# The last batch's end of a first attention inside the next block's programs, and low parts on another engine

## The chip, the cores and the metric

The kernel runs on one core of one Trainium2 chip. A core has TensorE (matrix products and transposes, results in PSUM), VectorE, ScalarE and GpSimd, each with its own program, and SyncE, whose queue starts the transfers. The engines meet at semaphores. The metric is the device time of one execution in microseconds (us), lower is better. In the profile PE is TensorE's matmuls, PEld its weight loads, DVE VectorE, ACT ScalarE, POOL GpSimd, SP SyncE.

## What is computed

Four transformer layers over 16 batches of 128 tokens, in float32. Layer 0 is an attention with 16 heads of 8 over 256 positions a batch and 128 channels, and a feed-forward. Layer 1 lets latents attend to the context and to themselves, with 16 heads of 16. Layer 2 has two cross attentions with 16 heads of 128. Layer 3 has a causal and a cross attention with 16 heads of 16. Cut to the parts that the change touches:

```python
# layer 0, per batch: q from x, k and v from the context
x = x + softmax(q @ k.T / sqrt(8)) @ v @ Wo
x = x + gelu(layer_norm(x) @ W1 + b1) @ W2 + b2
# layer 1
k, v = split(concat(context, x) @ kv_w + kv_b)
x = rmsnorm(x + softmax(q @ k.T / 4 + mask) @ v @ out_w + out_b)
# layers 1, 2 and 3, at their ends
x = x + gelu(norm(x) @ w1 + b1) @ w2 + b2
```

## The kernel before

Each attention and each feed-forward is one block: a set of five engine programs. All engines meet between two blocks. Inside a block there are only semaphores.

**The order of the work in a block** is one list of steps (`Order`), and each engine's program runs those steps of the list that are its own, in the order of the list. In the attentions of layers 0, 1 and 3 the list is made by sorting: a table (`AT0`, `AT1`, `AT3`) gives each stage a time in units of one batch, a step's key is its batch plus that time (`order0`, `order1`), and of equal keys the one that the table names first goes first. In layer 1 the second half of a batch's exponents has -3.18 (`exponents`, four steps for each half), and the next batch's turned maxima, `neg_T_a`, have -4.18, so the two keys are equal but for rounding. In the list `neg_T_a` of the next batch stands behind the second half for batches 0 to 7 and ahead of it for batches 8 to 14. PSUM banks go round in rings (`Ring`), one bank for each job in the order of TensorE's steps.

**Layer 0's attention** (`attention0`) ends for each batch with a chain: `untangle` (8 transposes of the slots, L1146), `share` (divide by the sum, L1311 and L1315), `context_T` (2 transposes) and its copy `turned_T`, `out` (one product with Wo, L1160), `added` (plus the tokens, L1322), `back` (2 transposes, L1167) and its copy `back_a` (L1254), `stats_b`, `root_b` (GpSimd), `scaled_b` (L1344), `renormed` (2 transposes, L1174) and `renormed_a`, which writes the normalized tokens `nT` (L1260).

**Layer 0's feed-forward** (`feed_forward0`) goes over eight groups of 512 tokens, two batches of 256 each. VectorE splits the group's `nT` into a rounded high part and the rest (`split`, L259 and L261), TensorE multiplies twice with three products each (`up`, L114), ScalarE makes Gelu (L242), TensorE multiplies back (`down`, L224), VectorE adds to x (`add`, L267) and, in groups 1 to 4, makes the masks for layer 1. TensorE's order is up(0), then up(g + 1), down(g).

**The feed-forwards of layers 1 to 3** (class `Feed`, order `FEED_ORDER`) have four groups g of four batches. A product of two float32 matrices is made of three products of high and low parts. So ScalarE rounds quarters of the weights (`w1_high` L1871, `w2_high` L1877) and the rest is made as low part: `w1_low(0)` on VectorE (L1971), `w1_low(1..3)` (L1919) and `w2_low(0..3)` (L1924) on GpSimd. Then for each of eight f: `up` on TensorE (six products of 512 columns), `gelu` on ScalarE (high part L1886, full L1889), `h_split` on VectorE (`h_low`, L1981). Then four steps `down(g, n)` of 24 products each, every one followed by `added` on VectorE (L1989), which needs `biased(b)` of its batch: GpSimd adds the bias row to x (L1948), with no wait but, in layers 2 and 3 at batch 12, for the scaled tokens. In layers 2 and 3 the normalization of the last group's tokens is made inside the block (`late_...`: statistics, root on GpSimd, scaling L2025, two turns L2069), and in layer 2 also that of group 0 for the layer behind (`early_...`: `early_stats` and `early_root` after `up(1, 1)`, `early_scaled` L2016 after `up(1, 4)`, in the list ahead of the last three `h_split` of group 1). Layer 2 takes its token parts from the attention and makes no `split`. In layer 1 GpSimd runs `split_context` after its steps of the list (L2713 and L2716, each twice, 2048 columns), for layer 2. At the end of every block GpSimd clears the semaphores of the block before (`clear_stale`). In the page's and the trace's names `l_mlp_...` stands for the feed-forwards' tiles.

## Time and profile before

| what | us |
|---|---|
| median of three runs (2301.53 to 2304.23) | 2302.02 |
| the profiled execution, its own time | 2303.46 |
| its span, from first to last instruction | 2301.4 |
| PE busy (share of the span) | 2161.2 (94%) |
| PEld busy | 1793.4 (78%) |
| DVE busy | 1479.8 (64%) |
| ACT busy | 1277.5 (56%) |
| POOL busy | 684.6 (30%) |

The blocks lie in the span like this: layer 0's attention to 328, its feed-forward to 358, layer 1's attention to 610, its feed-forward to 714, layer 2's attentions to 1786, its feed-forward to about 1890, layer 3's attentions to 2196, its feed-forward to the end at 2301.

A share is a mean over stretches with different limits, so it is only a first look. The timeline gives for each instruction or merged row of instructions its start, its duration, engine, line, operation, tiles with shapes and count, and in brackets how long the engine was idle before it and what it waited for. Rows of one engine alone merge otherwise than rows of all. `PEq` as releaser is the meeting of the engines between blocks. Matmul ends are modelled; the start of the next is the safer number.

### The profile page before, as it was taken

How to read it: one execution, taken by the hardware profiler on the slowest of the kernel's cores; microseconds unless marked ns; L12 is line 12 of the kernel's file. 1: busy time of each engine (PE TensorE's matmuls, PEld its weight loads, DVE VectorE, ACT ScalarE, POOL GpSimd, SP SyncE). 2: the span in 40 equal slices, each digit the busy share in tenths (PEclk: the TensorE clock that was granted, in tenths of full speed). 3: DMA queues.
4: the chain of work that ended last, by engine and by line, in shares of the span. 5: the costliest groups of instructions: out<-in, count | busy, mean ns of one | idle time of the engine just before them, and what ended most of it. 6: DMA issues, size and time to landing. Idle time of an engine off the chain costs nothing. (4 is left out here: it accounts for less than half of the span.)

```text
span 2301.4 us, 47738 instructions
## 1 busy us (share of the span) xinstructions
PE 2161.2 (94%) x18208; PEld 1793.4 (78%) x18208; DVE 1479.8 (64%) x2807; ACT 1277.5 (56%) x3300; POOL 684.6 (30%) x682
## 2 busy tenths in 40 slices
PE   6999979998798999999999999999998899999889
PEld 4666646877687888888888888888887786776678
DVE  5888744555454765666666666666666539999963
ACT  4777754555534444444445444444444448888853
POOL 5344310111433422030303312030101507677740
PEclk9999999999899999999999999999999999999999
DMA  3000020000102000010100001000000210000000
GB/s 133 16 16 11 2 56 1 2 2 2 38 1 78 24 24 24 10 38 1 47 1 19 29 17 31 10 28 1 1 1 32 79 35 23 2 2 2 2 10 28
DMA packets 33661, 50.58 MB, mean 22 GB/s; under 512 B 2592, under 2 KB 22048, under 8 KB 32416
## 3 DMA queue, kind: packets, MB, share of 16 engines
q1 hardware_dynamic: 33440, 47.53, 6.9%
q8 instruction: 151, 2.47, 0.5%
q14 instruction: 70, 0.57, 0.1%
HBM read 45.43 MB, written 2.10 MB: 21 GB/s over the span
## 5 line engine op out<-in xcount | busy, mean ns | idle before, releaser
L690 ACT ACTIVATE l_probs<-l_s_psum,l_neg_max 128x129 f32<-128x129 f32 x512 | 181.7, 368 | 267.7 <-DVE l_neg_max L753 267.7
L777 DVE TENSOR_TENSOR x<-x,l_o_psum 128x512 f32<-128x512 f32 x256 | 176.2, 688 | 189.9 <-PE l_o_psum L644 187.9
L522 POOL TENSOR_TENSOR l_head_w_high<-l_head_raw,one 128x768 fp32r<-128x768 f32 x30 | 44.5, 1483 | 516.9 <-PE l_o_psum L644 516.9
L675 ACT ACTIVATE l_KT<-l_k_psum,cols 128x512 f32<-128x512 f32 x128 | 88.2, 689 | 198.0 <-PE l_k_psum L114 198.0
L1303 DVE TENSOR_REDUCE l_neg_max<-l_psum 128x2 f32<-128x512 f32 x256 | 163.5, 683 | 46.5 <-PE l_psum L1093 46.2
L2365 POOL TENSOR_TENSOR l_probs<-l_probs,l_mask_add 128x512 f32<-128x512 f32 x128 | 161.9, 1287 | 76.2 <-DVE l_probs L2593 76.2
L644 PE MATMUL l_o_psum<-l_head_w_high,l_context_low 128*128 128x256 f32 x512 | 155.6, 304 | 8.8 <-DVE l_context_low L758 8.8
L758 DVE SCALAR_TENSOR_TENSOR l_context_low<-l_c_psum,cols,l_context_high 128x512 fp32r<-128x512 f32 x128 | 95.8, 749 | 105.5 <-ACT l_context_high L682 104.7
L2535 ACT ACTIVATE l_probs<-l_probs,l_neg_max 128x128 f32<-128x128 f32 x512 | 159.8, 396 | 5.4 <-DVE l_neg_max L2600 5.0
L1232 ACT ACTIVATE l_PT<-l_psum 128x512 f32<-128x512 f32 x256 | 132.2, 602 | 54.6 <-PE l_psum L1121 54.6
L644 PE MATMUL l_o_psum<-l_head_w_high,l_context_high 128*128 128x256 f32 x512 | 144.4, 282 | 5.1 <-DVE x L777 3.1
L630 PEld LDWEIGHTS l_c_psum<-l_PT,values 128*128 128x128 f32 x1024 | 134.4, 192 | 12.5 <-DVE l_PT L749 1.9
L644 PE MATMUL l_o_psum<-l_head_w_low,l_context_high 128*128 128x256 f32 x512 | 143.5, 280 | 0.0
L768 DVE TENSOR_TENSOR values<-l_v_psum,l_value_rows 128x512 f32<-128x512 f32 x128 | 88.5, 691 | 84.8 <-PE l_v_psum L114 83.4
L630 PE MATMUL l_c_psum<-l_PT,values 128*128 128x128 f32 x1024 | 136.0, 276 | 0.9 <-DVE l_PT L749 0.8
L610 PE MATMUL l_s_psum<-l_KT,l_QT 128*128 128x129 f32 x1024 | 135.8, 275 | 0.8 <-ACT l_QT L669 0.8
L1886 ACT ACTIVATE l_mlp_h_high<-l_mlp_psum,cols 128x512 fp32r<-128x512 f32 x96 | 66.3, 690 | 121.3 <-PE l_mlp_psum L114 114.8
L1981 DVE TENSOR_TENSOR l_mlp_h_low<-l_mlp_h,l_mlp_h_high 128x512 fp32r<-128x512 f32 x96 | 87.3, 924 | 69.3 <-ACT l_mlp_h L1889 69.1
L669 ACT ACTIVATE l_QT<-l_q_psum,l_query_bias 128x512 f32<-128x512 f32 x128 | 88.3, 690 | 76.6 <-PE l_q_psum L114 76.6
L610 PEld LDWEIGHTS l_s_psum<-l_KT,l_QT 128*128 128x128 f32 x1024 | 124.8, 191 | 1.4 <-ACT l_QT L669 1.2
L114 PE MATMUL l_mlp_psum<-l_mlp_w_high,l_mlp_h_high 128*128 128x256 f32 x384 | 111.7, 291 | 8.3 <-DVE l_mlp_h_low L1981 8.3
L114 PE MATMUL l_v_psum<-l_value_w_high,ctx_high 128*128 128x512 f32 x256 | 112.3, 439 | 7.5 <-DVE l_value_w_low L798 6.8
(303 smaller groups left out, 6403.0 us busy)
## 6 DMA issues: line engine op xcount, KB each, us to landing
l_head_raw<-in_l_heads SPq DMA_DIRECT2D x32, 384.0 KB, 3.1
l_w<-in_l_w SPq DMA_DIRECT2D x4, 1024.0 KB, 9.9
l_ctx_in<-in_ctx_T SPq DMA_DIRECT2D x16, 256.0 KB, 5.4
l_value_raw<-in_l_values SPq DMA_DIRECT2D x8, 512.0 KB, 3.6
l_value_rows<-in_l_rows SPq DMA_DIRECT2D x8, 512.0 KB, 5.2
l_x_in<-in_x_T SPq DMA_DIRECT2D x16, 128.0 KB, 2.2
l_x_in<-in_ctx_T SPq DMA_DIRECT2D x16, 128.0 KB, 2.5
values<-in_l_w SPq DMA_DIRECT2D x2, 1024.0 KB, 6.2
```

The lines of the kernel that those rows point to most:

```text
L114: last = pe.matmul(out, left[a], right[b], start=(start and n == 0), stop=(stop and n == 2))
L610: last = pe.matmul(scores[:, i // 2, i % 2, :], QT[:, i * S:(i + 1) * S], KT[:, i, :], start=True, stop=True)
L630: last = pe.matmul(c_bank[:, i * S:(i + 1) * S], V[:, u % 2, i, hh * P:(hh + 1) * P], PT[:, i * S:(i + 1) * S], start=True, stop=True)
L644: last = pe.matmul(o_bank[:, i % 2 * D:(i % 2 + 1) * D], context[left][:, i * S:(i + 1) * S], wo[right], start=(m == 0), stop=(m == 2))
L690: last = act.activation(probs[:, i, :], scores[:, i // 2, i % 2, :], ACT.Exp, bias=neg_max[:, i:i + 1], scale=1.0, accum_out=den[:, i:i + 1])
L758: dve.scalar_tensor_tensor(out=context[1][:, :], in0=c_bank[:, :], scalar=vector("bias_v", s), in1=context[0][:, :].bitcast(F32), op0=ALU. ...
L768: dve.tensor_tensor(out=V[:, u % 2, i, :], in0=v_bank[:, :], in1=value_rows[:, u // 4 % 2, 0, :], op=ALU.add).then_inc(v_free, 1)
L777: dve.tensor_tensor(out=x, in0=x, in1=o_bank[:, :], op=ALU.add).then_inc(o_free, 1)
L1232: act.activation(PT[:, 2 * w + t, g, :], score_banks[g][:, :], ACT.Exp).then_inc(exp_done, 1)
L1303: dve.tensor_reduce(neg_max[:, u % 2, qt, at:at + 2], bank[:, :].rearrange("p (e k) -> p e k", e=2), AX, ALU.max, negate=True).then_inc(fr ...
L2365: pool.tensor_tensor(out=probs[:, s % SCORES3, :, :], in0=probs[:, s % SCORES3, :, :], in1=four(mask_add[:, mask_slot(u), :]), op=ALU.add) ...
L2535: last = act.activation(p, p, ACT.Exp, bias=neg_max[:, s % SCORES3, m:m + 1], scale=1.0)
```

## The change

1. Layer 0's attention no longer has the last batch's steps from `untangle` on (`ENDING0`). They stand in `feed_forward0`, in a new class `Ending0`, with two further PSUM banks: TensorE untangles after up(0), turns the context after down(0), multiplies by Wo after down(1), turns back after down(2), turns the normalized tokens after down(4). ScalarE copies after its steps of groups 1, 3 and 5, VectorE's and GpSimd's steps are between theirs, and the split of the last group waits for the normalized tokens. The slots and the tokens live on in SBUF for it.
2. In layer 1's attention the second half of the exponents has -3.2 instead of -3.18, so it stands ahead of the next batch's `neg_T_a` for every batch. No other engine's order changes.
3. In the three `Feed` blocks all low parts of the weights are made on VectorE: `w1_low` where they stood, `w2_low(0..3)` after the `h_split` of f = 1 to 4 of group 0. One semaphore fewer.
4. GpSimd's `biased` of a group's first batch waits until the group's last up (f = 7) is done. Everything behind it in GpSimd's program waits with it: in layer 2 `late_low`, `early_root`, in layer 1 `split_context`.

```diff
--- before.py
+++ after.py
+class Ending0:
...
+    def untangle(self, pe):
+        for qt, bank in enumerate((self.first, self.second)):
+            for j in range(4):
+                at = j % 2 * 2 * S + qt * P
+                last = pe.transpose(bank[:, j * P:(j + 1) * P], self.c.slots0[:, j // 2, at:at + P], self.c.ident[:, :])
+            last.then_inc(self.untangled, 1)
+
+    def context_T(self, pe):
+        pe.wait_ge(self.shared, 2)
+        for qt in range(2):
+            last = pe.transpose(self.first[:, qt * P:(qt + 1) * P], self.ctx_q[:, qt, :], self.c.ident[:, :])
+        last.then_inc(self.context_turned, 1)
+
+    def make_out(self, pe):
+        pe.wait_ge(self.ctx_T_done, 1)
+        pe.matmul(self.second[:, 0:2 * S], self.c.w["l0_wo"][:, 0, :], self.ctx_T[:, :], start=True, stop=True)\
+            .then_inc(self.out_made, 1)
...
+    def copy_ctx_T(self, act):
+        act.wait_ge(self.context_turned, 1)
+        act.activation(self.ctx_T[:, :], self.first[:, 0:2 * S], ACT.Copy).then_inc(self.ctx_T_done, 1)
...
+    def share(self, dve):
+        for qt, bank in enumerate((self.first, self.second)):
+            dve.wait_ge(self.untangled, qt + 1)
+            slot = bank[:, :].rearrange("p (j m n) -> p m j n", j=4, m=4)
+            by_head = self.rden[:, qt, :, :].rearrange("p (m j) n -> p m j n", m=4)
+            dve.reciprocal(by_head, slot[:, :, :, 8:9]).then_inc(self.rden_done, 1)
+            dve.wait_ge(self.rden_done, qt + 1)
+            dve.tensor_tensor(out=self.ctx_q[:, qt, :].rearrange("p (m j d) -> p m j d", m=4, j=4),
+                              in0=slot[:, :, :, 0:8], in1=by_head.to_broadcast([P, 4, 4, 8]), op=ALU.mult)\
+                .then_inc(self.shared, 1)
...
+    def root(self, pool):
+        pool.wait_ge(self.var_done, 1)
+        inverse_root(pool, self.c, self.rstd_part, 0, self.mean_var[:, :, 1:2], self.rstd[:, :, :], 1e-5, 2)\
+            .then_inc(self.rstd_done, 1)
...
             up(0)
+            ending.untangle(pe)
             for g in range(groups):
                 if g + 1 < groups:
                     up(g + 1)
                 down(g)
+                if g == 0:
+                    ending.context_T(pe)
+                if g == 1:
+                    ending.make_out(pe)
+                if g == 2:
+                    ending.back(pe)
+                if g == 4:
+                    ending.renormed(pe)
...
+                if g == 1:
+                    ending.copy_ctx_T(act)
+                if g == 3:
+                    ending.copy_back(act)
+                if g == 5:
+                    ending.norm(act)
...
+            ending.root(pool)
...
+                if g == groups - 1:
+                    dve.wait_ge(ending.normed, 1)
...
             split(0)
             split(1)
+            ending.share(dve)
             for g in range(groups):
                 if g + 2 < groups:
                     split(g + 2)
+                if g == 4:
+                    ending.scale(dve)
                 add(g)
+                if g == 1:
+                    ending.add(dve)
+                if g == 3:
+                    ending.statistics(dve)
                 if 1 <= g < 5:
                     c.ahead1.masks(dve, masks_loaded, g - 1)
...
+ENDING0 = ("untangle", "share", "context_T", "turned_T", "out", "added", "back", "back_a", "stats_b", "root_b", "scaled_b",
+           "renormed", "renormed_a")
...
         for stage, at in AT0.items():
+            if u == B - 1 and stage in ENDING0:
+                continue
...
-        tokens = sb("tokens", [P, 4, 2 * KEYS])
+        tokens = c.tokens0
...
-    "exponents": (-4.15, -4.11, -3.97, -3.97, -3.18, -3.18, -3.18, -3.18),
+    "exponents": (-4.15, -4.11, -3.97, -3.97, -3.2, -3.2, -3.2, -3.2),
...
-        self.w1_first = sem("w1_first")
...
     def gpsimd(self, pool):
-        def w1_low(q):
-            if q == 0:
-                return
-            raw, high, low = self.quarter1(q)
-            pool.wait_ge(self.w1_rounded, q + 1)
-            pool.tensor_tensor(out=low, in0=raw, in1=high.bitcast(F32), op=ALU.subtract).then_inc(self.w1_ready, 1)
-
-        def w2_low(q):
-            raw, high, low = self.quarter2(q)
-            pool.wait_ge(self.w2_rounded, q + 1)
-            pool.tensor_tensor(out=low, in0=raw, in1=high.bitcast(F32), op=ALU.subtract).then_inc(self.w2_ready, 1)
-
...
         def biased(b):
             x = self.c.x[:, b, :]
+            if b % 4 == 0:
+                self.filled(pool, "up", b // 4, 7)
             if self.late and b == 12:
                 pool.wait_ge(self.xn_done, 1)
...
         def w1_low(q):
-            if q == 0:
-                raw, high, low = self.quarter1(0)
-                dve.wait_ge(self.w1_rounded, 1)
-                dve.tensor_tensor(out=low, in0=raw, in1=high.bitcast(F32), op=ALU.subtract).then_inc(self.w1_first, 1)
+            raw, high, low = self.quarter1(q)
+            dve.wait_ge(self.w1_rounded, q + 1)
+            dve.tensor_tensor(out=low, in0=raw, in1=high.bitcast(F32), op=ALU.subtract).then_inc(self.w1_ready, 1)
+
+        def w2_low(q):
+            raw, high, low = self.quarter2(q)
+            dve.wait_ge(self.w2_rounded, q + 1)
+            dve.tensor_tensor(out=low, in0=raw, in1=high.bitcast(F32), op=ALU.subtract).then_inc(self.w2_ready, 1)
 
...
         def up(g, f):
-            if f < 2:
-                pe.wait_ge(self.w1_first, 1)
-            else:
-                pe.wait_ge(self.w1_ready, f // 2)
+            pe.wait_ge(self.w1_ready, f // 2 + 1)
...
 FEED_ORDER = [("split", 0, 0), ("w1_high", 0), ("w1_low", 0), ("split", 0, 1), ("late_stats",)]
 for _q in range(1, 4):
     FEED_ORDER += [("w1_high", _q), ("w1_low", _q)] + ([("late_root",)] if _q == 1 else [])
-for _q in range(4):
-    FEED_ORDER += [("w2_high", _q), ("w2_low", _q)]
+FEED_ORDER += [("w2_high", _q) for _q in range(4)]
 for _g in range(4):
     FEED_ORDER += [("biased_b2", 4 * _g + _n) for _n in range(4)]
     for _f in range(8):
         FEED_ORDER += [("up", _g, _f), ("gelu", _g, _f), ("h_split", _g, _f)] + LATE_AT.get((_g, _f), [])
+        FEED_ORDER += [("w2_low", _f - 1)] if _g == 0 and 1 <= _f <= 4 else []
...
-                    with nc.sbuf_tensor("pos", [P, 4, P], F32) as pos:
-                        c.pos = pos
-                        attention0(c)
                     with ExitStack() as one:
-                        c.ahead1 = Ahead1(c, lambda n, shape, dt=F32: one.enter_context(nc.sbuf_tensor(f"l1_{n}", shape, dt)))
-                        feed_forward0(c)
+                        with ExitStack() as zero:
+                            c.slots0 = zero.enter_context(nc.sbuf_tensor("l0_slots", [P, 2, BANK], F32, side="right"))
+                            c.tokens0 = zero.enter_context(nc.sbuf_tensor("l0_tokens", [P, 4, 4 * S], F32, side="right"))
+                            with nc.sbuf_tensor("pos", [P, 4, P], F32) as pos:
+                                c.pos = pos
+                                attention0(c)
+                            c.ahead1 = Ahead1(c, lambda n, shape, dt=F32:
+                                              one.enter_context(nc.sbuf_tensor(f"l1_{n}", shape, dt)))
+                            feed_forward0(c)
```

## Rows read from the trace of the kernel before

**Rows 1.** Timeline, ScalarE, end of first attention: start, duration, engine, line, operation [idle before].

```profile
318.90 0.38 ACT L1254 ACTIVATE l_r<-l_psum 128x256 f32<-128x256 f32 x1
...
323.75 0.39 ACT L1254 ACTIVATE l_r<-l_psum 128x256 f32<-128x256 f32 x1 [1.74 <-DVE l_rn L1344]
...
328.27 0.42 ACT L236 ACTIVATE l_mlp_w_high<-l_w 128x256 fp32r<-128x256 f32 x1 [0.29 <-PEq L892]
```

**Rows 2.** Windows, same place: length, busy PE, PEld, DVE, ACT, POOL, granted clock, DMA.

```profile
324.00:328.00 4.00, 0.93 (x4) 0.29 (x2) 1.35 (x6) 1.26 (x3) 0.89 (x2) 0.57 0.00 0
...
330.00:334.70 4.70, 4.62 (x11) 3.69 (x12) 2.26 (x4) 1.75 (x3) 2.89 (x7) 0.50 0.99 333
```

**Rows 3.** Timeline, TensorE, first feed-forward: one group's second product.

```profile
347.55 1.88 PE L224 MATMUL l_mlp_psum<-l_mlp_hT,l_w 128*128 128x512 f32 x4
```

**Rows 4.** Timeline, ScalarE, second layer's attention, batches 6 to 10 and 14.

```profile
460.33 2.42 ACT L1701 ACTIVATE l_PT<-l_psum,l_mask_col 128x512 f32<-128x512 f32 x4 [0.52 <-PE l_psum L1601]
...
468.65 2.06 ACT L1701 ACTIVATE l_PT<-l_psum 128x512 f32<-128x512 f32 x4 [1.99 <-PE l_psum L1601]
...
474.25 2.42 ACT L1701 ACTIVATE l_PT<-l_psum,l_mask_col 128x512 f32<-128x512 f32 x4 [0.73 <-PE l_psum L1601]
...
487.49 2.42 ACT L1701 ACTIVATE l_PT<-l_psum,l_mask_col 128x512 f32<-128x512 f32 x4 [0.52 <-PE l_psum L1601]
...
498.16 0.28 ACT L1693 ACTIVATE l_neg_T<-l_psum 128x128 bf16<-128x128 bf16 x1 [4.34 <-PE l_psum L1580]
...
503.85 2.42 ACT L1701 ACTIVATE l_PT<-l_psum,l_mask_col 128x512 f32<-128x512 f32 x4 [0.74 <-PE l_psum L1601]
...
517.74 2.42 ACT L1701 ACTIVATE l_PT<-l_psum,l_mask_col 128x512 f32<-128x512 f32 x4 [0.52 <-PE l_psum L1601]
...
586.27 0.28 ACT L1693 ACTIVATE l_neg_T<-l_psum 128x128 bf16<-128x128 bf16 x1 [3.98 <-PE l_psum L1580]
```

**Rows 5.** Timeline, TensorE and VectorE, layer 1's feed-forward and the next block's start.

```profile
615.47 0.79 PE L114 MATMUL l_mlp_psum<-l_mlp_n_high,l_mlp_w_high 128*128 128x512 f32 x1 [1.46 <-DVE l_mlp_n_low L1964]
...
643.05 14.89 DVE L1981 TENSOR_TENSOR l_mlp_h_low<-l_mlp_h,l_mlp_h_high 128x512 fp32r<-128x512 f32 x7 [2.27 <-ACT l_mlp_h L1889]
...
671.20 0.69 DVE L1981 TENSOR_TENSOR l_mlp_h_low<-l_mlp_h,l_mlp_h_high 128x512 fp32r<-128x512 f32 x1 [2.27 <-ACT l_mlp_h L1889]
...
704.71 0.42 DVE L1989 TENSOR_TENSOR x<-x,l_mlp_psum 128x256 f32<-128x256 f32 x1 [0.88 <-PE l_mlp_psum L114]
...
714.09 1.41 DVE L727 BATCH_NORM_STATS2 l_stats<-x 128x6 f32<-128x256 f32 x4 [0.32 <-PEq L2110]
```

**Rows 6.** Timeline, GpSimd, layer 1's feed-forward: the context split's first two steps.

```profile
637.53 3.60 POOL L2713 TENSOR_TENSOR ctx_high<-ctx_raw,one 128x2048 fp32r<-128x2048 f32 x1
...
641.22 4.62 POOL L2716 TENSOR_TENSOR ctx_low<-ctx_raw,ctx_high 128x2048 fp32r<-128x2048 f32 x1
```

**Rows 7.** Timeline, layer 2's feed-forward: TensorE, GpSimd, ScalarE.

```profile
1799.83 0.66 PE L2069 MATMUL l_mlp_psum<-ident,l_mlp_xn 128*128 128x128 f32 x4 [1.76 <-DVE l_mlp_xn L2025]
...
1809.12 2.83 POOL L1948 TENSOR_TENSOR x<-x,rows 128x256 f32<-128x256 f32 x4
...
1823.76 1.34 POOL L104 TENSOR_TENSOR l_mlp_rstd<-l_mlp_rstd,minus_half 128x4 f32<-128x4 f32 x1
...
1844.62 0.69 ACT L1886 ACTIVATE l_mlp_h_high<-l_mlp_psum,cols 128x512 fp32r<-128x512 f32 x1 [15.87 <-PE l_mlp_psum L114]
```

**Rows 8.** Timeline, layer 3's feed-forward: ScalarE and VectorE.

```profile
2201.41 0.69 ACT L1886 ACTIVATE l_mlp_h_high<-l_mlp_psum,cols 128x512 fp32r<-128x512 f32 x1
...
2209.05 9.18 DVE L1981 TENSOR_TENSOR l_mlp_h_low<-l_mlp_h,l_mlp_h_high 128x512 fp32r<-128x512 f32 x7
...
2230.52 0.69 ACT L1886 ACTIVATE l_mlp_h_high<-l_mlp_psum,cols 128x512 fp32r<-128x512 f32 x1 [13.62 <-PE l_mlp_psum L114]
...
2252.94 0.69 ACT L1886 ACTIVATE l_mlp_h_high<-l_mlp_psum,cols 128x512 fp32r<-128x512 f32 x1 [11.63 <-PE l_mlp_psum L114]
...
2296.39 0.42 DVE L1989 TENSOR_TENSOR x<-x,l_mlp_psum 128x256 f32<-128x256 f32 x1 [2.46 <-PE l_mlp_psum L114]
```

More of the change, by code:

```diff
@@ L188, in feed_forward0 @@
         n_parts = [sb(f"n_{n}", [P, 2, BANK], F32R) for n in ("high", "low")]
-        psum = [ctx.enter_context(nc.psum_tensor(f"l0_mlp_psum{i}", [P, BANK], F32)) for i in range(6)]
+        psum = [ctx.enter_context(nc.psum_tensor(f"l0_mlp_psum{i}", [P, BANK], F32)) for i in range(8)]
         up_banks, down_banks = psum[0:4], psum[4:6]
@@ L195, in feed_forward0 @@
         masks_loaded, ctx_loaded, ahead_made = sem("masks_loaded"), sem("ctx_loaded"), sem("ahead_made")
+        ending = Ending0(c, sb, sem, psum[6:8])
         ctx.callback(hand_over, c, held, sems)
@@ L918, in attention0 @@
         PT = sb("PT", [P, 4, 4, BANK])
-        slots = sb("slots", [P, 2, BANK])
+        slots = c.slots0
         rden = sb("rden", [P, 2, H, 1])
@@ L1948, in biased @@
             pool.tensor_tensor(out=x, in0=x, in1=self.c.row(self.finish), op=ALU.add).then_inc(self.x_biased, 1)
-        return {"w1_low": w1_low, "w2_low": w2_low, "biased_b2": biased, "late_root": late_root, "late_low": late_low,
+        return {"biased_b2": biased, "late_root": late_root, "late_low": late_low,
                 "early_root": early_root}
@@ L2029, in late_scaled @@
             last.then_inc(self.xn_done, 1)
-        return {"split": split, "w1_low": w1_low, "h_split": h_split, "added_b2": added, "late_stats": late_stats,
+        return {"split": split, "w1_low": w1_low, "w2_low": w2_low, "h_split": h_split, "added_b2": added, "late_stats": late_stats,
                 "late_scaled": late_scaled, "early_stats": early_stats, "early_scaled": early_scaled}
```

54 lines of the change are left out of this document (added).

## The prediction

> **What bounds the kernel now.** I first read the busy shares: TensorE is busy 94% of the span, so only the stretches where it waits, or works at half clock, can give anything back. The page's chain that ended last covers only the end, so I went to the timeline at each place that the diff touches.
>
> At the end of the first attention the reader is to see a chain of short steps with nothing beside it: batch 15's residual is copied back at 323.75, and ScalarE starts the feed-forward at 328.27; batch 14's was copied at 318.90 [rows 1]. TensorE's granted clock falls to its lower level there (0.57 on average over 324 to 328, 0.50 at the start of the feed-forward) [rows 2].
>
> In the second layer's attention I read when ScalarE starts the first-half exponents of each batch [rows 4]. Batches 6 to 8 start at 460.33, 474.25 and 487.49: 13.92 and 13.24, a pair in 27.16. Batches 8 to 10 start at 487.49, 503.85 and 517.74: 16.36 and 13.89, a pair in 30.25. From batch 8 on, `neg_T_a` of the next batch stands before the second-half exponents and waits 4.34 (3.98 in batch 14) for TensorE [rows 4].
>
> In the feed-forwards one undisturbed group of four batches takes 22.42 (2230.52 to 2252.94 in layer 3) [rows 8]. Layer 1's second group takes 28.15 from its first `h_low` to the next group's, and seven of its `h_low` take 14.89 where one alone takes 0.69 [rows 5]; GpSimd runs the context split beside them [rows 6]. Layer 3's first group takes 29.11, seven `h_low` 9.18 [rows 8]: GpSimd works on low parts and biases there.
>
> **First layer: minus 1.6.** Removed from the first attention: the last batch's end. Next late there is batch 14's end, of the same steps: 4.52 from its copy to the next block, so 318.90 + 4.52 = 323.42 instead of 328.27, 4.85 earlier [rows 1]. The feed-forward gets it on TensorE, which is the bound of that stretch: 14 transposes, at most 0.66 / 4 = 0.165 each (four took 0.66) [rows 7], 2.3; the output matmul, 256 columns, two passes of half of 1.88 / 4, 0.5 [rows 3]. `renormed` in group 4 waits for VectorE's add, statistics, masks, split of group 6 and scaling; I estimate 0.4 of waiting, since this chain is about as long as TensorE's up and down. Together 3.2, between 2 and 4.9. The half-clock start moves with the block [rows 2]: I take the same cost; TensorE idles less, so it could also save one or two. VectorE's `share` and `added` and ScalarE's copies lie beside TensorE's up; the new wait of the last split for `normed` holds only `add` of group 5 and the last up behind it, which TensorE reaches after one up and one down. GpSimd's root queues ahead of clearing semaphores only.
>
> **Second layer's order: minus 13.2.** For batches 8 to 14 the second-half exponents now go ahead of the next `neg_T_a`, as they already do in batches 0 to 7; all other engines keep their order. Behind them waits `neg_T_a`, and the next batch's score on TensorE for it; in batches 6 and 7 just this order runs in 27.16 a pair. From batch 8 to 13 that is three times 16.36 - 13.92 = 2.44 and twice 13.89 - 13.24 = 0.65: 8.6. Batches 13 and 14 have no further projections to fill with; between 0.65 and the wait of 3.98 I take 2.3 each, as the steady case with the long wait has 2.4. Sum 13.2, between 9.9 and 16.6 [rows 4].
>
> **Layer 1's feed-forward: plus 0.6.** (a) The low parts of the first weights leave GpSimd, so VectorE's second token split is not slowed and TensorE's wait of 1.46 goes [rows 5]; the uninterrupted start may bring full clock sooner. I take 2.3, between 0 and 3. The seven low parts cost VectorE 0.69 each, in gaps that it has beside ups of 1.36; without that cover 4.8. (b) GpSimd's biases wait for the last up of their group, and the context split, queued behind all of them, moves out of group 1: 28.15 - 22.42 = 5.7 gained [rows 5, 8]. (c) It now stands at the block's end. The last up ends one down step before the add at 704.71; three more steps end at 713.35, so a step is 2.88 and the up ends at 701.83, 12.26 before the next block's 714.09 [rows 5]. From there GpSimd needs 2.83 for four biases [rows 7], 2 x (3.60 + 4.62) = 16.4 for the split [rows 6], some 0.4 for gaps and 0.3 to the next block, and then, uncovered for the first time, the clearing of twenty semaphores. No row shows a clearing. After the last add (2296.39) there are 5.0 to the span's end, with one store and some thirty clearings [rows 8], so one costs at most 0.17; I take 0.05, 1.0 in all (0 to 3.4). Sum 20.9 against 12.26: 8.6 lost. The half clock of the next block's start is there already, as TensorE starts it after a pause either way. 8.6 - 5.7 - 2.3 = 0.6. The same bound over 29 clearings at the second attention's end, 16 of them new, could cost up to 2.4; I take nothing, since they lie beside the last normalization's chain.
>
> The Trainium skill, page SBUF — State Buffer, section Summary: rules for kernel authors, says that a VectorE instruction with two inputs in SBUF and a GpSimd instruction that reads SBUF exclude each other, and the one that issues second waits until the other ends. The 14.89 above agree. By that rule the first bias at the tail could wait for the last `h_low`, and the tail would cost up to 0.7 more than by the row of four biases.
>
> **Layer 2's feed-forward: plus 0.9.** The first group gets rid of TensorE's wait of 1.76 for the scaled tokens, which VectorE computes against GpSimd's low parts [rows 7], and of slowed `h_low`; I take 2.2, between 0 and 3. But `early_root` is queued on GpSimd behind the biases of group 1, which now wait for that group's last up. VectorE's `early_scaled` stands before three `h_low` and waits for it. Counted from the last up: four biases 2.83, root about 1.7 with its first add, four scalings of 0.42 (taken from the add at 704.71, of the same width), three `h_low` of 0.69, the last products 0.4: 8.7 where a down step is 2.88 [rows 5, 7]. That is 5.8 of waiting, most of it one pause, so some 1.5 of half clock after it: 7.3. Today this group is 15.87 - 11.63 = 4.24 long of the undisturbed one [rows 7, 8]. Plus 3.1, between 0 and 5; the cover of the biases elsewhere is the down phase, 11.5.
>
> **Layer 3's feed-forward: minus 5.0.** First group 29.11 - 22.42 = 6.7 too long [rows 8], 1.0 of it the two turns. VectorE then has per up only 0.69, and 0.69 more in four of them, plus four scalings at 0.42: it no longer bounds. Part of the rest is the half clock at the start, which stays; but the first split is quicker too. Between 2 and 6.5; I take 5.0, nearer to the excess. GpSimd's end is hidden here.
>
> **Sum.** -1.6 - 13.2 + 0.6 + 0.9 - 5.0 = -18.3. The profiled execution took 2303.46 (span 2301.4), 1.4 over the median of 2302.02. The profiled one would take 2285.2, the median 2283.7.
>
> **Rivals.**
> - GpSimd does not matter. The slow `h_low` come from ScalarE's pace, or VectorE's own low parts now bound the first groups. Then 2.3, 2.2 and 5.0 are not gained: 2283.7 + 9.5 = 2293.2. For it: VectorE was full in these groups. Against: 9.18 for seven, at 0.69 alone [rows 8]. 9%.
> - The attention's rhythm changes at batch 8 for another reason: 2283.7 + 13.2 = 2296.9. Against: the 4.34 wait stands just there, and nothing else in the order changes. 4%.
> - Held GpSimd queue costs more: clearings at 0.17 (2.4 here, 2.4 at the attention's end), layer 2's stall at 5 instead of 3.1: 2290.4. 8%.
> - Slower than before: `neg_T_a`, now behind the exponents' 2.06 [rows 4], holds the next score in all seven batches. It decides if TensorE reaches that score before `neg_T_a` is done; then seven times 2.06 = 14.4 are lost instead of 13.2 gained: 2283.7 + 27.6 = 2311.3. Against: batches 6 and 7. 2%.
>
> **How the numbers follow.** The forecast has 77%. Its range takes the bounds of the unknown costs, which hardly all fall on one side: 2276.5 to 2291; this takes in the third rival, and leaves out the other 15% and the far ends. A measurement here tells about 0.2% (4.6) from no change. All cases but the last are faster by more: with a little for mishaps, 95% faster, 3% the same, 2% slower.
>
> **What would show it.** Right: first exponents of batches 8 to 13 about 27.2 a pair; seven `h_low` near their own 0.69 in layer 3's first group; group 1 of layer 1 at 22.4; about 21 between its last up and the next block, with GpSimd alone at the end; a TensorE pause of 5 in layer 2's second group; the first feed-forward starting 4.9 earlier and lasting 3 longer. Wrong: pairs still at 30.25, or a first group still above 27.

## The result and the profile after

The changed kernel took 2285.52 us, median of 4 runs (2281.77 to 2286.55), beside 2302.62 for the kernel before on the same chip: a ratio of 0.9922 (95% interval 0.9905 to 0.9939). A second measurement, made together with the variants below, gave 2282.18 in 5 runs and 0.9913 (0.9900 to 0.9926). The forecast was 2283.7. The profiled execution took 2285.99, its span 2283.4, so 18.0 less than before's span; the sum in the prediction said 18.3.

Stretch by stretch, from block start to block start. The last column takes the mean length over the profiled kernels of this study that have the edit, less the mean over those that lack it: 8 and 4 for the first three rows; 3 and 3 for the others (the changed kernel, its repeat and e3 against before, e1 and e2), since the other six have half of the feed-forward's edit or more than all of it. The repeat's profile shows how far one kernel differs from itself: 1.8 in the second layer's attention, 0.7 in layer 1's first group and 1.5 in layer 2's second. I had expected under 0.3 in the groups.

| stretch | forecast | before, after | difference | over all profiles |
|---|---|---|---|---|
| start of the first feed-forward | -4.85 | 328.27, 323.54 | -4.7 | -4.8 |
| its length | +3.2 | 30.20, 31.99 | +1.8 | +1.9 |
| second layer's attention | -13.2 | 252.07, 238.73 | -13.3 | -15.3 |
| layer 1's feed-forward | +0.6 | 103.55, 104.54 | +1.0 | +0.8 |
| layer 2's attention | 0 | 1071.79, 1073.59 | +1.8 | +0.4 |
| layer 2's feed-forward | +0.9 | 105.96, 105.65 | -0.3 | +1.3 |
| third attention | 0 | 303.90, 304.37 | +0.5 | +0.8 |
| layer 3's feed-forward | -5.0 | 105.65, 100.96 | -4.7 | -4.2 |

Changed kernel, timeline of ScalarE (columns as in rows 1). The first lines answer to [rows 1], the others to [rows 4].

```profile
319.03 0.38 ACT L1392 ACTIVATE l_r<-l_psum 128x256 f32<-128x256 f32 x1
...
323.54 0.42 ACT L352 ACTIVATE l_mlp_w_high<-l_w 128x256 fp32r<-128x256 f32 x1 [0.29 <-PEq L1030]
...
486.13 2.42 ACT L1839 ACTIVATE l_PT<-l_psum,l_mask_col 128x512 f32<-128x512 f32 x4 [0.52 <-PE l_psum L1739]
...
496.81 0.28 ACT L1831 ACTIVATE l_neg_T<-l_psum 128x128 bf16<-128x128 bf16 x1 [0.29 <-PE l_psum L1718]
...
500.05 2.42 ACT L1839 ACTIVATE l_PT<-l_psum,l_mask_col 128x512 f32<-128x512 f32 x4 [0.73 <-PE l_psum L1739]
...
565.43 2.42 ACT L1839 ACTIVATE l_PT<-l_psum,l_mask_col 128x512 f32<-128x512 f32 x4 [0.52 <-PE l_psum L1739]
...
572.30 0.28 ACT L1831 ACTIVATE l_neg_T<-l_psum 128x128 bf16<-128x128 bf16 x1
```

Batch 14's copy to the next block is 4.51, as [rows 1] had it for batch 15. From batch 8 on `neg_T_a` comes behind the second-half exponents and waits 0.29 where it waited 4.34 [rows 4]; batches 8 and 9 start 13.92 apart.

Changed kernel, layer 1's feed-forward, timeline of VectorE: the answer to [rows 5].

```profile
624.51 0.69 DVE L2112 TENSOR_TENSOR l_mlp_h_low<-l_mlp_h,l_mlp_h_high 128x512 fp32r<-128x512 f32 x1 [2.27 <-ACT l_mlp_h L2026]
...
634.04 1.18 DVE L2112 TENSOR_TENSOR l_mlp_h_low<-l_mlp_h,l_mlp_h_high 128x512 fp32r<-128x512 f32 x1 [0.67 <-ACT l_mlp_h L2026]
635.14 0.94 DVE L2089 CAST l_mlp_n_high<-nT_early 128x512 fp32r<-128x512 f32 x1
636.12 1.11 DVE L2091 TENSOR_TENSOR l_mlp_n_low<-nT_early,l_mlp_n_high 128x512 fp32r<-128x512 f32 x1
...
690.22 0.42 DVE L2120 TENSOR_TENSOR x<-x,l_mlp_psum 128x256 f32<-128x256 f32 x1 [2.46 <-PE l_mlp_psum L114]
698.80 1.41 DVE L859 BATCH_NORM_STATS2 l_stats<-x 128x6 f32<-128x256 f32 x4 [8.16 <-PEq L2238]
```

The same stretch on GpSimd, the answer to [rows 6].

```profile
632.78 3.90 POOL L2075 TENSOR_TENSOR x<-x,rows 128x256 f32<-128x256 f32 x4 [18.90 <-PE l_mlp_psum L114]
...
678.38 3.71 POOL L2075 TENSOR_TENSOR x<-x,rows 128x256 f32<-128x256 f32 x4 [18.90 <-PE l_mlp_psum L114]
682.05 3.60 POOL L2841 TENSOR_TENSOR ctx_high<-ctx_raw,one 128x2048 fp32r<-128x2048 f32 x1
...
693.98 4.49 POOL L2844 TENSOR_TENSOR ctx_low<-ctx_raw,ctx_high 128x2048 fp32r<-128x2048 f32 x1
```

The context split no longer lies beside the `h_low`; it follows the last group's biases. The last add ends at 690.64, VectorE waits 8.16 for GpSimd, and TensorE's last product lies 8.6 before the next block. From the last up (678.3) to the next block it is 20.5, where I had worked out 20.9. GpSimd's last operation ends at 698.47 and the next block starts at 698.80, so the twenty semaphore clearings, priced at 1.0 and "uncovered", cost nothing. The trace has them, in the view of their source line:

```profile
L66 POOLq EVENT_SEMAPHORE_RANGE_CLEAR  x20: 44/44/44, 693.9 to 695.3; - x20
```

They are 0.07 apart, issued by GpSimd's sequencer (`POOLq`) while its engine works on the last `ctx_low` (693.98 to 698.47). The price of one was near, but they are covered. New, and not in the prediction: the first bias lies beside the group's last `h_low`, which takes 1.18 instead of 0.69.

Changed kernel, timeline of ScalarE: first `h_high` of group 1 in layer 1, of group 2 in layer 2, and of groups 1 and 2 in layer 3 (the answers to [rows 7] and [rows 8]).

```profile
623.22 0.69 ACT L2023 ACTIVATE l_mlp_h_high<-l_mlp_psum,cols 128x512 fp32r<-128x512 f32 x1 [12.01 <-PE l_mlp_psum L114]
...
1830.06 0.69 ACT L2023 ACTIVATE l_mlp_h_high<-l_mlp_psum,cols 128x512 fp32r<-128x512 f32 x1 [17.89 <-PE l_mlp_psum L114]
...
2211.44 0.69 ACT L2023 ACTIVATE l_mlp_h_high<-l_mlp_psum,cols 128x512 fp32r<-128x512 f32 x1 [11.39 <-PE l_mlp_psum L114]
...
2234.23 0.69 ACT L2023 ACTIVATE l_mlp_h_high<-l_mlp_psum,cols 128x512 fp32r<-128x512 f32 x1 [12.00 <-PE l_mlp_psum L114]
```

Undisturbed groups wait 12.01 instead of 11.63 and take 22.80 instead of 22.42. Layer 2's second group waits 17.89 where [rows 7] had 15.87. Why, GpSimd and VectorE show.

```profile
1810.94 2.80 POOL L2075 TENSOR_TENSOR x<-x,rows 128x256 f32<-128x256 f32 x4 [16.61 <-PE l_mlp_psum L114]
1813.70 0.20 POOL L102 TENSOR_TENSOR l_mlp_rstd<-l_mlp_mean_var,epsilons 128x4 f32<-128x4 f32 x1
1813.98 1.02 POOL L104 TENSOR_TENSOR l_mlp_rstd<-l_mlp_rstd,minus_half 128x4 f32<-128x4 f32 x1
```

```profile
1815.03 1.67 DVE L2147 SCALAR_TENSOR_TENSOR l_mlp_xn<-x,l_mlp_mean_var,l_mlp_rstd 128x256 f32<-128x256 f32 x4 [6.22 <-POOL l_mlp_rstd L104]
1816.62 1.89 DVE L2112 TENSOR_TENSOR l_mlp_h_low<-l_mlp_h,l_mlp_h_high 128x512 fp32r<-128x512 f32 x3
```

The root stands behind the held biases, VectorE waits 6.22 for it, and three `h_low` that TensorE's down needs stand behind that. TensorE's own pause is 4.80:

```profile
1817.45 0.55 PE L114 MATMUL l_mlp_psum<-l_mlp_w_high,l_mlp_h_high 128*128 128x256 f32 x1 [4.80 <-DVE l_mlp_h_low L2112]
```

### The profile page after: what moved, and what is told of

It is laid out like the page before. It is cut to its first block and busy times, and to the rows that moved or that the text cites. A ratio compares the mean times of both kernels' runs of the same rounds, so it can differ in the third digit from the quotient of the medians.

```text
span 2283.4 us, 47741 instructions
## 1 busy us (share of the span) xinstructions
PE 2156.4 (94%) x18208; PEld 1791.3 (78%) x18208; DVE 1465.7 (64%) x2828; ACT 1277.7 (56%) x3300; POOL 653.0 (29%) x661
## 5 line engine op out<-in xcount | busy, mean ns | idle before, releaser
L890 DVE SCALAR_TENSOR_TENSOR l_context_low<-l_c_psum,cols,l_context_high 128x512 fp32r<-128x512 f32 x128 | 95.8, 748 | 105.3 <-ACT l_context_high L814 104.5
L114 PE MATMUL l_v_psum<-l_value_w_high,ctx_high 128*128 128x512 f32 x256 | 112.8, 441 | 15.4 <-DVE l_value_w_low L930 14.8
L776 PEld LDWEIGHTS l_o_psum<-l_head_w_high,l_context_low 128*128 128x128 f32 x512 | 96.5, 188 | 26.8 <-DVE l_context_low L890 24.1
L2112 DVE TENSOR_TENSOR l_mlp_h_low<-l_mlp_h,l_mlp_h_high 128x512 fp32r<-128x512 f32 x96 | 71.0, 742 | 71.4 <-ACT l_mlp_h L2026 71.2
```

The lines of the kernel that those rows point to most:

```text
L114: last = pe.matmul(out, left[a], right[b], start=(start and n == 0), stop=(stop and n == 2))
L776: last = pe.matmul(o_bank[:, i % 2 * D:(i % 2 + 1) * D], context[left][:, i * S:(i + 1) * S], wo[right], start=(m == 0), stop=(m == 2))
L890: dve.scalar_tensor_tensor(out=context[1][:, :], in0=c_bank[:, :], scalar=vector("bias_v", s), in1=context[0][:, :].bitcast(F32), op0=ALU. ...
```

## The experiments

First the change in its three parts, each by itself in the kernel before.

**The order alone (e1_order).**

```
-    "exponents": (-4.15, -4.11, -3.97, -3.97, -3.18, -3.18, -3.18, -3.18),
+    "exponents": (-4.15, -4.11, -3.97, -3.97, -3.2, -3.2, -3.2, -3.2),
```

> The kernel before with one edit alone: the second-half exponents of the second layer go ahead of the next batch's neg_T_a from batch 8 on. Forecast: 13.2 us less than before (bounds 9.9 to 16.6), first-half exponents of batches 8 to 13 in 68.2 instead of 76.9, of 13 to 15 in 21.5 instead of 27.6. Rival 2 (the rhythm changes at batch 8 for another reason): no change, 76.9 stays. In the changed kernel's trace batch 1 to 2 of this attention was 1.6 longer than before; if that comes from what stands in front of it (the first feed-forward), this kernel does not have it and saves 14.8; if it comes from the order itself, it has it and saves 13.2.

Measured: 2287.21, 0.9930 of before (0.9917 to 0.9942), so 16.1 less (13.4 to 19.1). The attention takes 237.07. Its ScalarE timeline:

```profile
498.62 0.28 ACT L1693 ACTIVATE l_neg_T<-l_psum 128x128 bf16<-128x128 bf16 x1 [0.28 <-PE l_psum L1580]
...
567.23 2.42 ACT L1701 ACTIVATE l_PT<-l_psum,l_mask_col 128x512 f32<-128x512 f32 x4 [0.52 <-PE l_psum L1601]
574.11 0.28 ACT L1693 ACTIVATE l_neg_T<-l_psum 128x128 bf16<-128x128 bf16 x1
577.64 2.42 ACT L1701 ACTIVATE l_PT<-l_psum,l_mask_col 128x512 f32<-128x512 f32 x4 [0.74 <-PE l_psum L1601]
```

Batches 8 to 13 take 68.2 and 13 to 15 21.5, as in the changed kernel; rivals 2 and 4 fall. Batch 1 to 2 takes 12.2 here as in before, so in its trace the part saves 15.0. The kernels with the ending in front show 12.2 to 15.5 there, and two without it (e3 13.8, e8 12.2) differ too. So that step is not set by the order; it varies with the clock: TensorE's granted clock is at its lower level there for none of the step where it takes 12.2, for 3.4 of it at 13.8 and for 6.8 at 15.5 (the changed kernel).

What came back is TensorE's idle time. TensorE's products of the exponents with V, in before (the last two steps, 13 to 14 and 14 to 15) and then in e1 (13 to 14):

```profile
573.89 3.52 PE L1615 MATMUL l_psum<-l_PT,l_V 128*32 128x128 f32 x64 [2.37 <-issue]
...
588.61 1.96 PE L1615 MATMUL l_psum<-l_PT,l_V 128*32 128x128 f32 x64 [2.37 <-issue]
```

```profile
563.29 1.95 PE L1615 MATMUL l_psum<-l_PT,l_V 128*32 128x128 f32 x64
```

They need the second-half exponents, which stand behind `neg_T_a` in before: at 571.73 they start, 2.06 later they are done, and at 573.89 TensorE goes on. From batch 8 on TensorE idles in before 2.37 and 0.59 by turns, then 2.37 in each of the last two steps. ScalarE's waits in these steps are 4.34 and 3.54 by turns, and 3.98 in the last. In e1 TensorE idles in none of these steps but 0.22 in the last, and the steps are shorter by 2.44, 0.65, then 4.0 and 2.15.

**The ending alone (e2_ending)**: the edits to the first attention, to the first feed-forward and to the two buffers that both use, nothing else.

> The kernel before with the last batch's end of the first attention moved into the first feed-forward, nothing else. Forecast: 1.6 less than before (4.85 earlier start, 3.2 longer feed-forward). By the traces of before and of the changed kernel: start 4.7 earlier, feed-forward 1.8 longer, so 2.9 less, or 1.4 if the longer batch 1 to 2 of the next attention comes from here. Rival: nothing is gained, because the feed-forward pays all of it back (0).

Measured: 2300.12, 0.9985 (0.9976 to 0.9994), 3.5 less (1.4 to 5.5). In its trace the block starts 3.8 earlier and lasts 32.16, 2.0 longer: 1.8. Over all profiles the start is 4.8 earlier and the block 1.9 longer: 2.9. Starts alone vary by 1.5 among kernels without this edit (328.27 to 329.80). The rival with 0 falls; between 1.4 and 2.9 this run does not decide.

**The feed-forward's part alone (e3_feed)**: low parts on VectorE, and the wait of the biases.

> The kernel before with the feed-forward's part alone: low parts on VectorE, and GpSimd's biases held until the last up of their group. Forecast: 3.5 less than before (+0.6, +0.9, -5.0). By the traces of the changed kernel: layer 1's feed-forward +1.0, the start of layer 2's attention +1.8 (TensorE's clock stays at its lower level longer after the longer pause), layer 2's feed-forward -0.3, third attention +0.5, layer 3's -4.7: 1.7 less. Rival 1 (GpSimd does not matter in the first groups): 6 more than before.

Measured: 2302.03, 0.9995 (0.9986 to 1.0004): 1.1 less, with no change inside the interval, so neither the 3.5 of the forecast (just outside it) nor a gain at all is shown. Its groups are those of the changed kernel (layer 1: 22.80, 22.80, and 29.98 from the last group's start to the next block; layer 2's second 28.82). The rival of 6 more falls. But this part pays itself back.

**The wait alone (e8_hold_only)**:

```
             x = self.c.x[:, b, :]
+            if b % 4 == 0:
+                self.filled(pool, "up", b // 4, 7)
```

> The kernel before with only the wait of GpSimd's biases for the last up of their group; the low parts stay on GpSimd. Theory A (the forecast's: GpSimd's low parts are what makes the first groups long): layer 1's second group 5.4 shorter, its tail 8.2 longer, its next block 1.8 longer, layer 2's second group 2 longer, the first groups as before; in all some 9 more than before. Theory B (the biases beside the h_low make the first groups long, not the low parts): first group of layer 3 6 shorter, of layer 2 3 shorter, and the time is as with the low parts moved, some 2 less than before.

Measured: 2309.61, 1.0027 (1.0016 to 1.0038), 6.2 more. Layer 1's second group is 22.80, its last stretch 29.99, layer 2's second group 29.2. Layer 3's first group is 27.1, where before has 29.1 and e3 23.6: of the 5.5, holding the biases gives 2.0 and moving the low parts then 3.5. Theory A holds for the larger part, B for the smaller. This split goes by the order in which the two edits are made: the next run, which moves the low parts and does not hold the biases, has 31.1 there, more than before. Its layer 3, VectorE and then GpSimd:

```profile
2210.27 5.83 DVE L2027 SCALAR_TENSOR_TENSOR l_mlp_xn<-x,l_mlp_mean_var,l_mlp_rstd 128x256 f32<-128x256 f32 x4
2216.02 8.63 DVE L1983 TENSOR_TENSOR l_mlp_h_low<-l_mlp_h,l_mlp_h_high 128x512 fp32r<-128x512 f32 x7
```

```profile
2209.70 3.24 POOL L1919 TENSOR_TENSOR l_mlp_w_low<-l_w,l_mlp_w_high 128x512 fp32r<-128x512 f32 x2
2212.90 6.04 POOL L1924 TENSOR_TENSOR l_mlp_w_low<-l_w,l_mlp_w_high 128x512 fp32r<-128x512 f32 x4
2219.64 4.46 POOL L1950 TENSOR_TENSOR x<-x,rows 128x256 f32<-128x256 f32 x4 [0.70 <-PE l_mlp_psum L114]
```

Four scalings take 5.83 beside GpSimd's low parts, 1.67 without (row at 1815.03 of the changed kernel).

**The changed kernel without the wait (e4_no_hold)**: the two lines above taken out again.

> The changed kernel without the wait of GpSimd's biases for the last up of their group; low parts stay on VectorE. Theory A (the wait costs more than it saves, as it did with the low parts on GpSimd, where it cost 6): 6 to 8 less than the changed kernel, about 2279: tail of layer 1 back to 12.3 from its last up, groups at 22.42, layer 2's second group under 25; the context split runs beside the h_low of layer 1's first two groups and costs some 5 there. Theory B (with the low parts on VectorE that engine has no slack left in the first groups, so biases beside it cost there what the wait saves): the same as the changed kernel, first groups of layers 2 and 3 at 26 or more.

Measured: 2295.46, 0.9968 (0.9955 to 0.9980), 13.3 more than the changed kernel measured beside it. Both theories miss it; B is nearer. Layer 2's second group is 26.7, and the tail is short again, but layer 1's first group takes 42.0 and layer 3's 31.1 (layer 2's 23.3, where B had 26 or more). Layer 1, GpSimd, VectorE and TensorE:

```profile
593.11 17.33 POOL L2073 TENSOR_TENSOR x<-x,rows 128x256 f32<-128x256 f32 x16 [2.81 <-POOLq L1564]
610.40 4.05 POOL L2839 TENSOR_TENSOR ctx_high<-ctx_raw,one 128x2048 fp32r<-128x2048 f32 x1
614.53 4.82 POOL L2842 TENSOR_TENSOR ctx_low<-ctx_raw,ctx_high 128x2048 fp32r<-128x2048 f32 x1
```

```profile
610.91 4.08 DVE L2100 TENSOR_TENSOR l_mlp_w_low<-l_w,l_mlp_w_high 128x512 fp32r<-128x512 f32 x1
614.92 13.90 DVE L2110 TENSOR_TENSOR l_mlp_h_low<-l_mlp_h,l_mlp_h_high 128x512 fp32r<-128x512 f32 x3
```

```profile
620.04 0.55 PE L114 MATMUL l_mlp_psum<-l_mlp_w_high,l_mlp_h_high 128*128 128x256 f32 x1 [8.27 <-DVE l_mlp_h_low L2110]
```

With its low parts gone GpSimd starts the context split sooner, and VectorE, which has more to do, gets one instruction through for each of GpSimd's long ones: 4.08 and then 13.90 for three. TensorE waits 8.27, 3.03 and 3.94, and its down products then run at the lower level of its clock (one every 0.21 instead of 0.12). Layer 3 has no context split; there sixteen biases in 16.78 lie beside VectorE's low parts and `h_low`, which take 1.22 each instead of 0.69. So neither half of the feed-forward's part can stand alone. The wait alone costs 6.2. The low parts without it cost about 12: e4 is 7.4 below before, with some 19 of gain from the other two parts. Together they give 1.1 (e3), which the interval doesn't tell from nothing.

Then what the held queue costs, one item after the other, from the changed kernel on.

**The context split spread out (e5_context)**:

```
-    FEED_ORDER += [("biased_b2", 4 * _g + _n) for _n in range(4)]
+    FEED_ORDER += [("biased_b2", 4 * _g + _n) for _n in range(4)] + [("beside", _g)]
```

(`beside` issues the n-th of the split's four instructions.)

> The changed kernel with the context split cut in its four instructions, one behind each group's biases, instead of all four behind the last group's. My theory (the tail's 20.5 is GpSimd's queue alone, and the down phases have room, 11.5 for biases of 3.7 and a part of 4.6): tail 8.2 shorter, next block 0 to 2 shorter at its start, 9 less than the changed kernel in all. Rival (a part beside the token split and the adds holds VectorE, and TensorE waits for a bank): groups 23.5 or more, and no more than 5 less in all.

Measured: 2276.83, 0.9884 (0.9871 to 0.9898), 5.4 less than the changed kernel beside it (0.9913), with intervals 0.0002 apart; 9 were expected. The profiled spans differ by 11.5, but e5's is the shortest of its 4 and the repeat's one of the two longest of its 5. Layer 1 takes 95.7 instead of 104.5 or 103.9, its last stretch 22.15 instead of 29.98: 7.8 of the 8.2 expected. Groups stay at 22.80, so the rival's mechanism falls, although the total is close to its 5 and VectorE is held for a whole part:

```profile
611.51 3.82 DVE L2089 CAST l_mlp_n_high<-nT_early 128x512 fp32r<-128x512 f32 x1
615.36 0.69 DVE L2091 TENSOR_TENSOR l_mlp_n_low<-nT_early,l_mlp_n_high 128x512 fp32r<-128x512 f32 x1
```

The cast takes 3.82 beside `ctx_high` (611.00 to 615.05), 0.42 alone; the adds come late and catch up, as TensorE has two more down products to do.

**All three mended (e7_after_h)**: the same, and

```
-                self.filled(pool, "up", b // 4, 7)
+                pool.wait_ge(self.h_ready, 2 * b + 8)
```

with `biased_b2` and `beside` behind the eight ups in the order, so that `early_root` is ahead of them.

> As the one before, and the biases stand behind the ups in the order, so that layer 2's early root is ahead of them on GpSimd, and they wait for the group's last h_low instead of its last up. My theory: groups back to 22.42 from 22.80 (three in each of three feed-forwards, 0.38 each, 3.4 to 4.2 in all), because the last h_low (1.18 beside a bias, 0.69 alone) is no longer slowed; layer 2's second group from 28.7 to about 24.2, 4.5 less. With the context split's 9: 17 less than the changed kernel, about 2268. Rival for the 0.38 (it comes from the slower splits behind the h_low, 0.94 and 1.11 instead of 0.43 and 0.69): the groups stay at 22.8, as the biases still lie beside the splits.

Measured: 2264.41, 0.9833 (0.9820 to 0.9846), 38 less than before and 18 less than the changed kernel: the best version here. Layer 2 on VectorE and GpSimd:

```profile
1794.92 1.67 DVE L2147 SCALAR_TENSOR_TENSOR l_mlp_xn<-x,l_mlp_mean_var,l_mlp_rstd 128x256 f32<-128x256 f32 x4
```

```profile
1793.37 1.34 POOL L104 TENSOR_TENSOR l_mlp_rstd<-l_mlp_rstd,minus_half 128x4 f32<-128x4 f32 x1
1799.17 2.83 POOL L2075 TENSOR_TENSOR x<-x,rows 128x256 f32<-128x256 f32 x4 [4.46 <-DVE l_mlp_h_low L2112]
```

No wait for the root is left; that group takes 22.42, better than the 24.2 expected, and undisturbed groups are back at 22.42. In layer 1 the splits still take up to 1.11 beside the biases, and the groups are 22.42 all the same: the 0.38 came from the last `h_low`, not from the splits.

**One of them undone (e6_root)**: e7 with the wait for the last up.

> The version with all edits behind the changed kernel (e7) with one of them undone: the biases wait for the group's last up again, not for its last h_low; the early root is ahead of them. My theory: layer 2's second group without its stall (22.8, where the changed kernel has 28.7 to 30.1), and every group 0.38 longer than in e7: in all 3.4 to 4.2 more than e7, about 2268.5. Rival (the held biases, not the root's place, make the stall): 28 or more in that group.

Measured: 2270.45, 0.9856 (0.9835 to 0.9876), 6.0 more than e7, which was measured on another chip (5.3 by the two ratios to before); groups at 22.80, layer 2's second at 22.86. So the stall there was the root's place alone, and 0.38 a group is the wait's. The three feed-forwards are 4.9 longer in the traces, 1.3 of it in one first group.

**The low parts alone, in the best setting (e9_low_on_gpsimd)**: e7 with `w1_low` (but for its first quarter) and `w2_low` on GpSimd.

> e7 with the low parts of the weights back on GpSimd, where before had them; the context split, the early root and the biases where e7 has them. My theory (the place of the low parts by itself is worth what the kernel with the held biases alone lacked in its first groups): layer 1 2.4 longer (start 6.6, first group 23.4), layer 2 2.6 longer, layer 3 3.6 longer (start and first group 32.8 instead of 29.2), 8.6 more than e7, about 2273. Rival (with GpSimd's biases out of the way its low parts cost nothing): as e7.

Measured: 2274.72, 0.9875 (0.9857 to 0.9893), 10.3 more than e7, or 9.7 by the ratios. In the traces layer 1 is 2.8 longer, layer 2 2.1, layer 3 2.9: 7.8 of the 8.6 expected; the other 3.2 between the two spans lie in blocks that the edit doesn't touch. The rival falls: the low parts by themselves cost this even with the biases out of the way. VectorE's scaling again takes 5.83:

```profile
2177.16 5.83 DVE L2165 SCALAR_TENSOR_TENSOR l_mlp_xn<-x,l_mlp_mean_var,l_mlp_rstd 128x256 f32<-128x256 f32 x4
```

## Why the prediction was right, point by point

- **First layer** (-1.6; traces -2.9, e2 alone -3.5). The start was right: 4.85 forecast, 4.7 to 4.8 found. The mis-sized term is the 3.2 of added TensorE work, found to be 1.9. Two things made it too large. I took a quarter of a row of four transposes, 0.66, as one's price; that row's length includes a latency once. Two of them take 0.38 here, the eight of `untangle` 1.31, the first part of it at the lower level of the clock. And TensorE came back to its full clock a little sooner: granted 0.50 for 6.5 from the start in before (as in [rows 2]), but for 5.1 in the changed kernel, which has 0.96 over 328.10 to 334.00. Over the profiles it is 5.4 with the edit and 6.5 without. Half of that time taken off each block's length leaves 29.5 in all eight kernels with the edit and 26.9 to 27.2 in the four without. So by this estimate 2.5 of the 3.2 was real work at full clock, and some 0.6 came back by the clock. The prediction named this as a possible one or two. `renormed` waits 0.31 for its scaled tokens, taken as 0.4:

```profile
328.07 1.31 PE L192 MATMUL l_mlp_psum<-ident,l_slots 128*128 128x128 f32 x8
...
332.32 0.38 PE L198 MATMUL l_mlp_psum<-ident,l_mlp_ctx_q 128*128 128x128 f32 x2
...
346.08 0.44 PE L216 MATMUL l_mlp_psum<-ident,l_mlp_rn 128*128 128x128 f32 x2 [0.31 <-DVE l_mlp_rn L262]
```

```profile
328.10:334.00 5.90, 5.90 (x28) 4.38 (x27) 3.48 (x9) 3.01 (x5) 0.20 (x2) 0.96 1.19 305
```

- **Second layer's order** (-13.2; traces -15.3, e1 alone -15.0 in its trace). The 8.6 for batches 8 to 13 is exact. The last two, taken at 2.3 each, gave 6.1 together: 4.0 from batch 13 to 14 and 2.15 from 14 to 15. The 4.0 looks like the wait of 3.98 [rows 4], the upper bound that I had named, but that wait lies in the other step, which gave 2.15. TensorE's rows above have it: 2.37 of idle time comes back in each (2.15 in the last, where 0.22 stay), and in the first of the two another 1.6, since the 64 products behind the pause took 3.52 at the lower level of the clock (granted 0.50 over 573.75 to 577.16) and take 1.95 without it. All four kernels without the edit have this (15.1 for that step), all eight with it 11.1. So 2.3 each was the right price of the pauses, and the clock behind one of them was missing from the sum. The changed kernel's own trace hid this: it lost 3.3 at batch 1 to 2 by the clock (15.5 against 12.2), and the repeat 1.6.
- **Layer 1's feed-forward** (+0.6; +0.8). All three terms hold: the start and first group 2.3 shorter (2.1 over the profiles), the second group 28.15 to 22.80, the tail 20.5 long against 20.9. Missing was 0.38 in each group. The prediction said that the biases' cover is the down phase, but they start with the last up's end and meet one more `h_low`.
- **Layer 2's feed-forward** (+0.9; -0.3 here, +1.3 over the profiles). First group 26.50 to 23.41: 3.1 instead of 2.2. TensorE's pause, worked out as 5.8, is 4.80, and just that in all five kernels whose root stands behind the held biases. The second group, 26.66 to 28.68, is 2.0 longer instead of 3.1, but it is 25.2 in e1 and e2 and 30.1 in the repeat, by where the lower clock level falls, so such a difference of two traces carries an error of some 2. Over the profiles it is 3.5 longer, so the 3.1 holds.
- **Layer 3's feed-forward** (-5.0; -4.2). Start and first group 5.75 shorter (5.3 over the profiles); the three other groups give back 1.1 by the same 0.38.
- **Clearings** (1.0 taken, none paid) were issued under GpSimd's last operation. The 2.4 of the third rival for sixteen of them is also too little for its own price (16 x 0.17 = 2.7).
- **Layer 2's attention**, forecast at no change, was 1.8 longer. The clock's lower level lasts to 714 there, 15 past the block's start:

```profile
710.00:714.00 4.00, 4.00 (x13) 3.24 (x12) 1.65 (x7) 1.00 (x3) 2.45 (x3) 0.50 0.11 45
714.00:718.00 4.00, 3.90 (x17) 2.82 (x15) 0.69 (x1) 2.22 (x5) 2.64 (x2) 0.96 0.00 0
```

I had argued that the half clock of that start "is there already". Measured to the seventh of ScalarE's operations, the block's start takes 15.7, 15.8, 15.6 and 14.8 with the 8 us pause in front (changed kernel, its repeat, e8, e3), and without it 14.0 to 14.3 in six kernels (before, e1, e2, e4, e6, e7), but 15.7 and 15.6 in e5 and e9. That length follows the time for which the granted clock is at its lower level in the block's first 16: 6.8 (before, e1, e2, e6, e7: 14.0 to 14.1), 10.2 (e4: 14.3), 12.3 (e3: 14.8), 13.7 (e5 and e9) and 14.8 to 15.5 (the changed kernel, its repeat, e8). So the argument failed: the half clock is there either way, but not equally long. The long pause had over 12 of it in all four kernels, the short one in two of eight; whether it costs 1.0 (the difference of the means) or up to 1.8, these runs do not settle.
- **Rivals.** The first fell by the first groups and by e9, the second and the fourth by e1. The third, that the held queue costs more, falls on both its terms: the clearings are covered, and layer 2's second group cost 3.5 and not 5. But the queue did cost more than was priced, by 0.38 a group, and e7 shows that all the waiting behind it was worth 18.

The last column adds up to -19.1, beside -18.3 forecast. Two terms gave 3.4 more than forecast (first layer 1.3, order 2.1), five gave 2.6 less (0.38 a group and the longer start of layer 2's attention among them). That these nearly cancel is luck; the mechanisms behind the large terms are the ones forecast.

## What to carry to other kernels

When a queue is held back by a wait, list all that stands behind it, and give each item its own place: here the same wait kept a 16 us split, a root that another engine waited for, and biases that needed to wait for one step more; placing the three was worth as much as the whole change. Two edits that relieve one engine pair should be measured together and apart, since each alone can cost what the other prevents (6 and 12 here, against a gain of 1). To price a wait that an edit removes, read the idle time of the engine that bounds the stretch, and what its clock does after it, not the wait of another engine. Here ScalarE's wait of 3.54 was worth 0.65 in one step and 4.0 in another; TensorE idled 0.59 in the first, and 2.37 with 1.6 of lower clock after it in the second. Look also whether a sequencer runs ahead of its engine, as GpSimd's did here with the clearings.

## What the runs showed of the hardware

VectorE and GpSimd held each other up by whole instructions: a cast of 128x512 from SBUF to SBUF took 0.42 alone, 0.94 beside biases and 3.82 beside a context part; three `h_low` took 13.90 beside three parts of 4 to 5; four scalings 1.67 alone and 5.83 beside low parts. The adds, with one input in PSUM, are not held: in e7 (VectorE, then GpSimd) one takes its 0.42 inside a context part.

```profile
615.91 0.42 DVE L2120 TENSOR_TENSOR x<-x,l_mlp_psum 128x256 f32<-128x256 f32 x1 [2.46 <-PE l_mlp_psum L114]
```

```profile
613.35 3.60 POOL L2843 TENSOR_TENSOR ctx_high<-ctx_raw,one 128x2048 fp32r<-128x2048 f32 x1
```

That the cast, with one input, is held as well was new to me. The Trainium skill, page SBUF — State Buffer, section Who interferes with whom, says this: a VectorE copy or cast in its two-port mode, or an instruction with two SBUF inputs beside a GpSimd instruction that reads SBUF, excludes the other and is excluded by it until the end, and one with a single SBUF input outside that mode is not. The rows agree with both halves, though no row names the mode.
